# An expert MLP over 128 sequences: x scaled and split one sequence further ahead, part of the rotation moved to ScalarE, a shorter root

## The reference, cut to what matters

```python
h = gelu(x @ Wi[e] + bi[e])          # 512 -> 2048, exact gelu
o = h @ Wo[e] + bo[e]                # 2048 -> 512
r = o + x
y = (r - mean(r)) / sqrt(var(r) + 1e-12) * gamma[e] + beta[e]
# then, on each group of four features of y:
out = [y0*ct + y1*st, -y0*st + y1*ct, y2*cp + y3*sp, -y2*sp + y3*cp]
```

## Time and profile before

| | |
|---|---|
| median of 3 runs | 3029.11 us (3025.92 to 3030.88) |
| the profiled execution | 3023.2 us, its span 3021.5 us |
| TensorE matmul busy | 2744.7 us, 91% of the span |
| VectorE busy | 2377.5 us, 79% |
| ScalarE busy | 887.4 us, 29% |
| GpSimd busy | 1603.3 us, 53% |
| TensorE clock granted, mean | 0.970 |
| first and last residual add (L648) | 111.9 us and 3009.4 us, 128 of them |

### The profile page before, as it was taken

One profiled execution on the slowest core, in us unless ns is written; L12 is line 12 of the kernel. 1 busy time (PEld: TensorE's weight loads), 2 busy tenths in 40 slices (PEclk: granted clock), 3 DMA queues, 4 the chain that ended last, 5 costly groups with the idle time before them and its releaser, 6 DMA issues.

```text
span 3021.5 us, 54615 instructions
## 1 busy us (share of the span) xinstructions
PE 2744.7 (91%) x12306; PEld 1220.8 (40%) x12307; DVE 2377.5 (79%) x5177; ACT 887.4 (29%) x1433; POOL 1603.3 (53%) x1619
## 2 busy tenths in 40 slices
PE   2888999889999989998999999999889989999998
PEld 1333444334444434433444444444334433444443
DVE  4688878877778887888877888878887788877777
ACT  4222332223332223322333222222223222233332
POOL 4879727973017974479700478706876479700000
PEclk9899999999999999999999999999999999999999
DMA  4546445655444655546544446545465546534343
GB/s 161 139 115 166 114 132 123 161 129 126 87 101 126 159 132 128 132 111 170 118 108 91 125 114 170 128 105 142 121 153 142 132 105 164 123 87 91 80 94 70
DMA packets 742560, 375.89 MB, mean 124 GB/s; under 512 B 682816, under 2 KB 682944, under 8 KB 733824
## 3 DMA queue, kind: packets, MB, share of 16 engines
q1 hardware_dynamic: 677568, 173.95, 29.9%
q0 software_dynamic: 25984, 130.29, 13.2%
q10 hardware_dynamic: 38976, 71.32, 7.3%
HBM read 174.13 MB, written 33.55 MB: 69 GB/s over the span
## 4 chain that ended last, share of the span: by engine, by line
PE 29%; DVE 29%; DMA 23%; issue 11%; DVEq 6%; ACTq 1%; POOL 1%; ACT 1%; SPq 0%; POOLq 0%
DMA xbuf<-in_x 16%; PE z_ps L825 15%; PE o_ps L841 14%; DVE h L638 7%; DMA hT<-h 5%; DVEq L195 3%; DVE xbuf L671 2%; DVE hid L627 2%; DVE x L632 2%; DVE ln L665 2%; DVE ln L667 2%; DVE xbuf L654 1%; DVE y L686 1%; DVE turned L683 1%; DMA xT<-x 1%
## 5 line engine op out<-in xcount | busy, mean ns | idle before, releaser
L825 PE MATMUL z_ps<-wi,xT 128*128 x6096 | 1449.0, 389 | 173.3 <-DMA xT<-x 119.5
L841 PE MATMUL o_ps<-wo,hT 128*128 x6144 | 1423.8, 382 | 47.7 <-DMA hT<-h 35.0
L825 PEld LDWEIGHTS z_ps<-wi,xT 128*128 128x128 f16 x6096 | 607.8, 100 | 945.7 <-issue 287.9
L841 PEld LDWEIGHTS o_ps<-wo,hT 128*128 128x128 f16 x6144 | 605.0, 98 | 791.0 <-issue 86.2
L471 ACT ACTIVATE hid<-hid 128x512 f32<-128x512 f32 x512 | 322.0, 629 | 1507.4 <-DVE hid L627 1506.2
L638 DVE SCALAR_TENSOR_TENSOR h<-hid,tok,h 128x512 f16<-128x512 f32 x512 | 494.4, 966 | 43.5 <-ACT h L479 31.0
L405 POOL TENSOR_TENSOR wi<-staged 128x512 f32<-128x512 f32 x112 | 133.8, 1195 | 650.1 <-DVE xbuf L648 639.1
L479 ACT ACTIVATE h<-hid,tok 128x512 f16<-128x512 f32 x512 | 369.6, 722 | 281.1 <-DMA hT<-h 262.0
L627 DVE SCALAR_TENSOR_TENSOR hid<-z_ps,tok,bi_all 128x512 f32<-128x512 f32 x512 | 382.2, 747 | 80.1 <-DVE y L686 28.1
L338 POOL TENSOR_SCALAR staged<-staged,wscale 128x512 f32<-128x512 f32 x224 | 197.7, 883 | 20.9
L646 DVE TENSOR_SCALAR ln<-inv,ex 128x1 f32 (+1 forms) x128 | 27.3, 214 | 211.5 <-issue 173.8
(11 more groups left out here) (124 smaller groups left out, 1771.3 us busy)
## 6 DMA issues: line engine op xcount, KB each, us to landing
staged<-in_L_cond_Wi POOLq DMA_DIRECT2D x56, 1024.0 KB, 5.7
staged<-in_L_cond_Wo POOLq DMA_DIRECT2D x56, 1024.0 KB, 6.1
xbuf<-in_x ACTq DMA_DIRECT2D x128, 256.0 KB, 2.7
out<-y ACTq DMA_DIRECT2D x128, 256.0 KB, 2.2
hT<-h SPq DMA_TRANSPOSE x512, 3.1
bi_all<-in_L_cond_bi POOLq DMA_DIRECT2D x7, 1024.0 KB, 7.5
wi<-in_L_cond_Wi SPq DMA_DIRECT2D x4, 1024.0 KB, 8.7
wo<-in_L_cond_Wo ACTq DMA_DIRECT2D x4, 1024.0 KB, 11.7
```

Source lines behind the costliest of these rows:

```text
L825: last = t.matmul(z_ps[:, n, :], xT16[:, j, a, k, :], wi16[:, bass.ds(b, 1), w, k, cs], start=(k == 0 and (a, w) == PASSES[0]), stop=(k == ...
L841: last = t.matmul(o_ps[:, j, :], hT16[:, n, a, c, :], wo16[:, bass.ds(b, 1), w, n * GC + c, :], start=(n == 0 and c == 0 and (a, w) == PAS ...
```

## The change

- `scale_x` and `hi_x` work one sequence further ahead: in turn s they handle s+2. `lo_x(s+1)` becomes VectorE's first vector instruction in the turn, and SyncE's x transpose is put ahead of the transpose of bank 3 of s-1. ScalarE fetches x of s+3 and sums s+2; `hi_x(s+2)` is its last arithmetic in the turn, after `gelu_bank` 3, which first waits for the x transpose of s+1.
- The rotation: ScalarE multiplies each pair of features by its cosine into `y` (`turn_own`, two instructions on 256 columns, after `gelu_bank` 2). VectorE then adds the sine products in four instructions, each on 128 columns that lie four apart (`rotate`, between `lo_group` 1 and `z_bank` 3). `rotate_products` and `rotate_sums` are gone.
- The root takes nine instructions: another start value, one Newton step with other constants and one step of higher order.
- At the start x of sequence 1 is summed, scaled and its hi half written early; the rotation tables have six columns in place of eight; `turned` shares room with `hid`.

```diff
@@ SyncE
+                if there(s, 1, inner):
+                    transpose_x(1 - k)
                 if there(s, -1, inner):
                     transpose_h(NB - 1)
-                if there(s, 1, inner):
-                    transpose_x(1 - k)
...
@@ ScalarE
-            def gelu_bank(s, k, n):
+            def gelu_bank(s, k, n, ahead):
                 hb = hid[:, n * BANK:(n + 1) * BANK]
+                if ahead and n == NB - 1:
+                    act.wait_ge(s_xT, (s + 2) * 16)
...
+            half = lambda ap, j: ap.rearrange("p (d f) -> p d f", f=4)[:, :, 2 * j:2 * j + 2]
+
+            def turn_own(s):
+                act.wait_ge(s_lnx, 1)
+                act.sem_clear(s_lnx)
+                for j in range(2):
+                    last = a.activation(half(y[:], j), half(x_of(s), j), ACT.Copy,
+                                        scale=rot[:, bass.ds(s, 1), j:j + 1].rearrange("p a n -> p (a n)"))
+                last.then_inc(s_turn, 1)
...
-                ahead, here = there(s, 1, inner), there(s, 0, inner)
-                if there(s, 2, inner):
-                    fetch_x(s + 2, k)
+                ahead, here = there(s, 2, inner), there(s, 0, inner)
+                if there(s, 3, inner):
+                    fetch_x(s + 3, 1 - k)
                 if ahead:
-                    sum_x(s + 1, 1 - k)
+                    sum_x(s + 2, k)
                 if here:
-                    gelu_bank(s, k, 0)
+                    gelu_bank(s, k, 0, ahead)
+                    gelu_bank(s, k, 1, ahead)
+                if there(s, -3, inner):
+                    act.wait_ge(s_y, (s - 2) * 16)
+                if here:
+                    gelu_bank(s, k, 2, ahead)
+                if there(s, -2, inner):
+                    turn_own(s - 2)
+                if here:
+                    gelu_bank(s, k, 3, ahead)
                 if ahead:
-                    hi_x(s + 1)
-                if here:
-                    for n in range(1, NB):
-                        gelu_bank(s, k, n)
+                    hi_x(s + 2)
                 if there(s, -2, inner):
                     store(s - 2)
...
@@ VectorE, root()
-                step(v.tensor_scalar(as_int(rstd), as_int(t), -1.0, float(0x5F3759DF), ALU.mult, ALU.add))
-                for _ in range(3):
-                    step(v.tensor_scalar(t, rstd, rstd, var, ALU.mult, ALU.mult))
-                    step(v.tensor_scalar(t, t, -0.5, 1.5, ALU.mult, ALU.add))
-                    step(v.tensor_scalar(rstd, rstd, t, None, ALU.mult))
+                step(v.tensor_scalar(as_int(rstd), as_int(t), -1.0, float(0x5F1FFFF9), ALU.mult, ALU.add))
+                step(v.tensor_scalar(t, rstd, rstd, var, ALU.mult, ALU.mult))
+                step(v.tensor_scalar(t, t, -0.703952253, 0.703952253 * 2.38924456, ALU.mult, ALU.add))
+                step(v.tensor_scalar(rstd, rstd, t, None, ALU.mult))
+                step(v.tensor_scalar(t, rstd, rstd, var, ALU.mult, ALU.mult))
+                step(v.tensor_scalar(os, t, 0.375, -1.25, ALU.mult, ALU.add))
+                step(v.tensor_scalar(t, t, os, 1.875, ALU.mult, ALU.add))
+                step(v.tensor_scalar(rstd, rstd, t, None, ALU.mult))
...
@@ VectorE, normalise()
-                v.scalar_tensor_tensor(out=xr, in0=xr, scalar=rstd, in1=row(bgb_all, b, (2, slice(None))), op0=ALU.mult, op1=ALU.add).then_inc(s_ln, 1)
+                v.scalar_tensor_tensor(out=xr, in0=xr, scalar=rstd, in1=row(bgb_all, b, (2, slice(None))), op0=ALU.mult, op1=ALU.add).then_inc(s_lnx, 1)
+                v.engine_nop().then_inc(s_ln, 1)
...
+            def rotate(s):
+                every = lambda ap, j: ap.rearrange("p (d f) -> p f d", f=4)[:, j, :]
                 xr = row(xbuf, s % XB)
+                dve.wait_ge(s_turn, s + 1)
+                for to, of, sine in ((0, 1, 2), (1, 0, 3), (2, 3, 4), (3, 2, 5)):
+                    last = v.scalar_tensor_tensor(out=every(y[:], to), in0=every(xr, of),
+                                                  scalar=row(rot, s, slice(sine, sine + 1)),
+                                                  in1=every(y[:], to), op0=ALU.mult, op1=ALU.add)
+                last.then_inc(s_done, 1)
...
@@ VectorE, iteration()
+                if ahead:
+                    lo_x(s + 1)
                 if last:
                     b2 = slot_value(dve, BUF, s - 2, 1)
                     residual(s - 2, k, b2)
...
                     z_bank(s, 0, b)
-                if ahead:
-                    scale_x(s + 1)
                 if back:
                     lo_group(s - 1, 1 - k, NB - 1)
...
                     z_bank(s, 1, b)
-                if ahead:
-                    lo_x(s + 1)
+                if there(s, 2, inner):
+                    scale_x(s + 2)
                 if here:
                     lo_group(s, k, 0)
-                if last:
-                    rotate_products(s - 2, inner)
                 if here:
                     z_bank(s, 2, b)
                     lo_group(s, k, 1)
                 if last:
-                    rotate_sums()
+                    rotate(s - 2)
                 if here:
                     z_bank(s, 3, b)
                     lo_group(s, k, 2)
```

More of the change, by code:

```diff
@@ L104, in expert_mlp_rotate_kernel @@
         y = sb("y", [P, H])
-        turned = sb("turned", [P, H])
-        rot = sb("rot", [P, S, 8])
+        rot = sb("rot", [P, S, 6])
         tab = sb("tab", [1, 3 * S + 2 * E + 1], I32)
@@ L144, in expert_mlp_rotate_kernel @@
         spread = hid[:, 1024:1024 + 4 * P]
+        turned = hid[:, 1536:1536 + BANK]
         s_idx = sem("s_idx")
@@ L188, in expert_mlp_rotate_kernel @@
         s_ln = sem("s_ln")
+        s_lnx = sem("s_lnx")
+        s_turn = sem("s_turn")
         s_done = sem("s_done")
@@ L314, in boot_bias @@
                     piece = bi_all[:, 0, n * BANK:(n + 1) * BANK]
-                    chain.step(g.tensor_tensor((y if n else turned)[:], piece, piece, ALU.mult))
+                    chain.step(g.tensor_tensor(y[:] if n else turned, piece, piece, ALU.mult))
                     if n:
-                        chain.step(g.tensor_tensor(turned[:], turned[:], y[:], ALU.add))
+                        chain.step(g.tensor_tensor(turned, turned, y[:], ALU.add))
                 w = BANK // 2
@@ L527, in _ @@
             sum_x(0, 0)
+            fetch_x(2, 0)
             squares(0, 1)
@@ L531, in _ @@
             squares(0, 3)
+            sum_x(1, 1)
             for q in range(Q):
@@ L537, in _ @@
             hi_parts(0)
+            act.wait_ge(s_xT, 16)
+            hi_x(1)
             for q in range(Q):
@@ L671, in normalise @@
                 step(v.scalar_tensor_tensor(out=xr, in0=xr, scalar=mean, in1=row(bgb_all, b, (1, slice(None))), op0=ALU.subtract, op1=ALU.mult))
-                v.scalar_tensor_tensor(out=xr, in0=xr, scalar=rstd, in1=row(bgb_all, b, (2, slice(None))), op0=ALU.mult, op1=ALU.add).then_inc(s_ln, 1)
[L674 to L680, removed]
-                xr = row(xbuf, s % XB)
[L682 to L691, removed]
+                v.scalar_tensor_tensor(out=xr, in0=xr, scalar=rstd, in1=row(bgb_all, b, (2, slice(None))), op0=ALU.mult, op1=ALU.add).then_inc(s_lnx, 1)
+                v.engine_nop().then_inc(s_ln, 1)
+            def rotate(s):
+                every = lambda ap, j: ap.rearrange("p (d f) -> p f d", f=4)[:, j, :]
+                xr = row(xbuf, s % XB)
+                dve.wait_ge(s_turn, s + 1)
[4 more added lines that the diff above has]
+                last.then_inc(s_done, 1)
             def iteration(s, k, inner=False):
@@ L771, in _ @@
             total(0)
+            scale_x(1)
             dve.wait_ge(s_sin, 1)
@@ L781, in _ @@
             dve.wait_ge(s_tabp, 2)
-            for col, src, sign in ((0, 0, 1), (1, 0, 1), (2, 1, 1), (3, 1, 1), (4, 2, -1), (5, 2, 1), (6, 3, -1), (7, 3, 1)):
+            for col, src, sign in ((0, 0, 1), (1, 1, 1), (2, 2, 1), (3, 2, -1), (4, 3, 1), (5, 3, -1)):
                 step(v.tensor_scalar(rot[:, :, col], o_ps[:, 0, src * S:(src + 1) * S], float(sign), None, ALU.mult))
```

## The result

The changed kernel takes 3357.8 us in the median of 4 runs (3354.6 to 3367.1), beside 3027.5 us for the kernel before: a ratio of 1.109, 95% interval 1.107 to 1.112. The forecast was 3156 us with a range up to 3260: the right sign, and outside the range by 98 us.

The account below looks back on a forecast made before the run. VectorE was taken to bound slow turns and, after the change, all turns: 69.6 slow turns at 25.5 us and 57.4 quick at 21.75 add 127 us, giving 3156 us, range 2990 to 3260.

Parts of the forecast that it names:

- What bounds the kernel: Whole kernel before: VectorE bounds slow turns outright, matches TensorE in quick ones; TensorE's 120 us xT wait mostly VectorE's lateness.
- slow turns: Turns while GpSimd loads an expert: 24.0 us each before, about 74 of 127; forecast 25.5 us after the change.
- quick turn: Turn without GpSimd loading: 21.17 us before, about 53 of 127; forecast 21.75 us after the change.
- rival 1: VectorE's wait at rotate: claimed covered, so faster, 2894 us, or about 2990 with half covered in slow turns; chance 0.19.
- The new wait: VectorE before rotate: waits for ScalarE's turn_own behind gelu_bank 2, idle 3.5 us; rotate begins at E + 4.95 in quick turns.
- E: In VectorE's turn, the end of lo_group 0; forecast 12.04 us into a quick turn, from which the chain is timed.
- the top of the turn: VectorE from lo_group 2 to L646: 2.9 us, register loads inside, against 3.20 before; 2.95 in the quick sum.
- The 16-byte step: VectorE's four rotate instructions, a new SBUF line at every element: estimated 0.53 us a turn, or nothing without the rule.
- rival 4: The four rotate instructions' 16-byte step costs 67 us on top: 3223 us; chance 0.17 together with the GpSimd rival.
- the central sum: Whole kernel: 69.6 slow turns at 25.5 us and 57.4 quick at 21.75, +127 us, median 3156 us; chance 0.47 for 3100 to 3200.
- Beside GpSimd: The four rotate instructions in slow turns: 0.44 us extra each, 2.8 us together; bounds no extra, 1.1, to 3.8.
- each high case: Slower than forecast: 16-byte step 3223 us, or short instructions waiting for GpSimd's 3220 to 3320; chance 0.17 together.

Follow-up runs that it names:

- e5: The kernel before with the new root alone: 2993 us, ratio 0.988.
- e12: The kernel before with x one further ahead, new root, third register load ahead of lo_x, hi_x(s+2) ahead of gelu_bank 3, old rotation: 2924 us, ratio 0.967.
- e1: The changed kernel with ScalarE's two cosine products ahead of gelu_bank 2 in place of behind it: 2982 us, ratio 0.987.
- e13: The changed kernel with room for four banks in h16 in place of two, nothing moved: 3048 us, ratio 1.008.
- e2: The changed kernel with VectorE's third register load put back ahead of lo_x: 3228 us, ratio 1.067.
- e4: The changed kernel with VectorE's four sine instructions on 128 adjacent columns in place of every fourth one: 3306 us, ratio 1.094.
- e3: The changed kernel with cosine products ahead of gelu_bank 2 and the third register load ahead of lo_x: 2939 us, ratio 0.971.
- e8: The kernel before with x one further ahead alone, rotation and root as before: 3139 us, ratio 1.037.

## Why the forecast had the sign and missed the size

**What bounds the kernel: right in the main.** VectorE's chain paced the slow turns: e5 takes some 0.45 us from it (0.50 in the timelines, since the instructions that go are one L665 and one L666) and gains 35 us. TensorE's waits for xT were in part VectorE's lateness, for e5 shortens them to 88.6 us without touching x. But starting x sooner has a worth of its own, 69 us from e5 to e12. The 21.17 us of a quick turn was also not TensorE's floor, as rival 1 took it: e1's quick turns average 20.7.

**The new wait: right in place and nearly in size.** The copy of bank 2 starts at E + 3.31 (3.35 forecast), `rotate` at E + 5.13 (4.95). The idle time is 514.3 / 128 = 4.0 us a turn, not 3.5. e1 takes it away and wins 376 us; e13 takes more than half of it away by other means and wins 310. That the sign was right is thus no luck.

**The step that failed: the top of the turn.** The forecast put L646's successor 0.66 us after `lo_x`, "with register loads inside it". The wait for `hi_x` stands in `lo_x`, and the third load stands behind `lo_x` in program order, so VectorE's sequencer reached it only when that wait was over, and there it took 1149 ns. I counted the loads as one block and did not ask which side of the moved wait each stood on. From `lo_group` 2 to L671 it is 4.16 us, not 2.95. e2 prices that at 130 us, two thirds of the 202 us missed.

**The 16-byte step was real.** It was rival 4, left out of the central sum, at 0.53 us a turn or 67 us. e4 measures 0.10 us for each of four instructions and 52 us. The Trainium skill (SBUF — State Buffer, section SBUF: two separate sides) says that each access that crosses to a new 16-byte line pays a penalty, and the 0.10 us agrees with it. Its price was below my estimate of twice the time for each element. Whether reading or writing pays was not separated.

**One turn, added up.** The turn in the timeline takes 23.24 us where the forecast's parts make 21.7. Up to E it is 0.19 shorter than forecast. Then `rotate` begins 0.18 late, its four instructions take 0.36 more, and the top of the turn 1.21 more. Over the whole kernel the gains of e2 and e4 leave some 20 us of the 202. But the wait's own excess, 0.5 us a turn, would be 64 us, so the prices do not simply add up, as e3 shows for the load; how the rest divides is open.

**Beside GpSimd: the right size, in part by luck.** In the slow window L709 took 28.76 us for 40 instructions, 0.72 each, and I had 2.8 us for the four of a turn. But without GpSimd each took 0.38 (13.76 / 36) and not 0.27, so GpSimd added 0.34 and not 0.44. The step that was left out made up for an addition taken too high.

**The range** ended at 3260 because each high case was priced alone. The load and the step occurred together, on top of the forecast. Rival 1's mechanism is what e1 shows: with the wait covered the kernel is faster, 2982 us, where the rival gave 2894 with the full gain and 2990 with half.

## What to carry to other kernels

When work is handed to an idle engine, look at what stands ahead of it in that engine's order, waits included, and follow the longest back: here it led to a DMA started by the engine that was to be relieved. When a wait is moved to the top of a loop, list which register loads stand ahead of it and which behind; those behind can't be hidden by it. Starting a transfer sooner pays only if no new wait takes the old one's place: x one further ahead cost 112 us as it stood in e8, and with the load and `hi_x` moved it gained 69 (e12 against e5).

## What was not expected of the hardware

A register load behind `lo_x` is slow. In the changed kernel's turn above, VectorE has one load between 1675 and 1678.2 us, which starts 0.1 us after `lo_x` does (duration in ns, min/median/max):

```profile
L197 DVEq TENSOR_LOAD <-tab x1: 1149/1149/1149, 1676.3 to 1676.3; - x1
```

In 24 turns in a row from there this load takes 0.9 to 1.16 us in 23, and 310 ns in one. Before the change the three loads of a turn took 306, 611 and 623 ns in one quick turn, and in e2 all three take 305 to 314. What makes such a load take 300 or 1149 ns was not tried.

A step of 16 bytes in fp32 costs VectorE 103 ns on 128 columns (453 against 350), while the old half-width sums with a step of 8 bytes took 0.420 us for 256 columns. From the full-width product to these the time falls by 1.04 ns a column (0.265 us for 256), as it does from 512 to 128 adjacent columns in the sine instructions' form (750 and 350 ns). So the step of 8 bytes shows no such price.
